# VectorE's weighted sum of three batches back, issued inside the rounds of the decode, and TensorE's side work moved behind unit 5

## What is computed

```python
h = jnp.maximum(_layernorm(x, axis=-1), 0.0)
h = h @ W
e = leaky_relu((h @ a_src)[:, None] + (h @ a_dst)[None, :], 0.2)
attention = softmax(where(adj > 0, e, NEG_INF), axis=1)
x = x + attention @ h
```

## Time and profile before

| | us |
|---|---|
| median of 3 executions | 851.71 (850.29 to 860.48) |
| the profiled execution, its device time | 860.06 |
| span in the profile of it | 858.3 |
| VectorE busy in it | 592.4 |

### The profile page before, as it was taken

The page is one execution under the profiler, slowest core; times in us unless marked ns, Lnnn a source line. Parts: engine busy times, 40 slices in busy tenths (PEclk is TensorE's granted clock), DMA queues, the critical chain, the costliest instruction groups (busy, mean ns, idle before and its releaser), DMA issues.

```text
span 858.3 us, 8941 instructions
## 1 busy us (share of the span) xinstructions
PE 445.4 (52%) x1823; PEld 213.9 (25%) x1855; DVE 592.4 (69%) x3125; ACT 525.0 (61%) x371; POOL 512.0 (60%) x522
## 2 busy tenths in 40 slices
PE   4787555555555546545554545475055567533421
PEld 3652222222222222212122222132022222211221
DVE  7956577777777767566678767767177788755784
ACT  3979777666767667766387777666154877732000
POOL 3745666666656665765655666667636665665571
PEclk9888678677676777766677777777578767765555
DMA  8999999999999999989599999999659799992110
GB/s 339 424 370 419 404 408 408 408 411 407 410 409 409 408 409 405 399 315 393 217 415 411 408 409 408 408 401 409 233 210 394 277 408 409 411 402 92 25 38 11
DMA packets 40903, 299.31 MB, mean 349 GB/s; under 512 B 11052, under 2 KB 14034, under 8 KB 24464
## 3 DMA queue, kind: packets, MB, share of 16 engines
q1 hardware_dynamic: 22976, 276.83, 79.3%
q0 software_dynamic: 15328, 17.58, 6.6%
q10 hardware_dynamic: 2544, 4.33, 1.5%
HBM read 304.31 MB, written 8.65 MB: 365 GB/s over the span
## 4 chain that ended last, share of the span: by engine, by line
DVE 72%; another core or an unknown queue 11%; issue 8%; PE 5%; ACT 2%; DMA 0%; POOLq 0%; DVEq 0%; ACTq 0%
DVE x_all L821 18%; DVE rest L638 5%; DVE words L636 5%; DVE words L640 4%; PE banks L1049 3%; DVE wf L666 2%; DVE top L680 2%; DVE top_bit L662 2%; DVE cand L676 2%; DVE cand L723 1%; DVE one_hot L768 1%; DVE e L785 1%; DVE top_bit L672 1%; DVE top L727 1%
## 5 line engine op out<-in xcount | busy, mean ns | idle before, releaser
L361 POOL DMA_INDIRECT gathered<-table,index x448 | 448.7, 1002 | 295.1 <-DVE index L714 151.4
L467 ACT ACTIVATE mask_buf<-adj_buf,minus_half 128x2048 bf16<-128x2048 int32 x252 | 489.5, 1992 | 141.3 <-issue 56.5
L1049 PE MATMUL banks<-mask_buf,bit_ident 128*128 128x512 bf16 x992 | 316.6, 472 | 37.6 <-issue 24.7
L821 DVE SCALAR_TENSOR_TENSOR x_all<-gathered,weight,x_all 128x128 f32<-128x128 f32 x512 | 157.5, 348 | 16.1 <-DVE x_all L821 7.6
L1049 PEld LDWEIGHTS banks<-mask_buf,bit_ident 128*128 128x128 bf16 x1024 | 113.2, 121 | 203.4 <-issue 137.6
L1061 PE MATMUL banks<-is_wide,before 128*128 128x1 bf16 x64 | 6.9, 176 | 207.9 <-DVE is_wide L751 155.9
L1090 PE MATMUL banks<-x_all,one_hot 128*128 128x128 f32 x128 | 35.4, 368 | 74.1 <-DVE x_all L821 39.0
L481 ACT ACTIVATE prob<-e 128x16 f32<-128x16 f32 x31 | 6.5, 208 | 103.6 <-issue 72.7
L636 DVE MAX8 words<-banks 128x8 f32<-128x512 f32 x64 | 44.3, 693 | 25.4 <-PE banks L1049 18.7
L1061 PEld LDWEIGHTS banks<-is_wide,before 128*128 128x128 bf16 x64 | 4.5, 112 | 227.8 <-DVE is_wide L751 170.8
L640 DVE MAX8 words<-rest 128x8 f32<-128x512 f32 x64 | 44.5, 695 | 2.4 <-DVE rest L638 0.2
(11 more groups left out here) (162 smaller groups left out, 589.4 us busy)
## 6 DMA issues: line engine op xcount, KB each, us to landing
adj_buf<-in_adj SPq DMA_DIRECT2D x128, 2048.0 KB
gathered<-table,index POOLq DMA_INDIRECT x448
table<-gathered ACTq DMA_DIRECT2D x4, 1040.0 KB, 14.0
x_all<-in_x SPq DMA_DIRECT2D x3, 1024.0 KB, 10.8
out<-x_all SPq DMA_DIRECT2D x2, 1280.0 KB
x_all<-in_x SPq DMA_DIRECT2D x2, 512.0 KB, 5.1
out<-x_all SPq DMA_DIRECT2D x1, 1024.0 KB
w_gathered<-table,w_index POOLq DMA_INDIRECT x24
```

The costliest lines, as they stand in the source:

```text
L361: nc.gpsimd.indirect_dma_start(g_cols[buf][:, k, :], None, table, bass.IndirectOffsetOnAxis(index[:, buf, k:k + 1], 0), bounds_check=N, oo ...
L467: nc.scalar.activation(mask_buf[:, u], adj_buf[:, u], ACT.Sign, bias=minus_half[:]).then_inc(mask_ready, 1)
L821: ins = v.scalar_tensor_tensor(at[b], g_view[par][b][:, k, 0:F], weight[:, b, k:k + 1], at[b], ALU.mult, ALU.add)
L1049: ins = mm(bank, bit_ident[:, h * PART_BITS + c], mask_buf[:, u, c * BIT_COLS:(c + 1) * BIT_COLS], start=False, stop=(h == PARTS - 1 and c ...
```

## The change

VectorE: in batches 3 to 29 the exponentials' sum, reciprocal and weights of batch i-3 (`weights`) run between the two `find_words`, each with a step of `logits(i-2)`, under `alone`; the eight pairs (`weighted`) follow `place_wide` as steps beside `decode(i)`. TensorE: records, counts and sums all stand behind unit 5, in that order, ahead of units 6 and 7. ScalarE: `wide_softmax` stands behind unit 7, not 5.

```diff
-                        if u == 5 and i == GROUP_ENDS[g] + 7:
+                        if u == UNITS - 1 and i == GROUP_ENDS[g] + 7:
                             wide_softmax(g)
...
+            def weights(i):
+                two = i % 2
+                dve.wait_ge(exp_ready, i + 1)
+                v.tensor_reduce(max_sum[:, i % BUFS, :, 1], prob[:, two], AX.X, ALU.add)
+                yield
+                v.reciprocal(r4[:], max_sum[:, i % BUFS, :, 1])
+                yield
+                v.tensor_tensor(weight[:], prob[:, two], r4[:].unsqueeze(2).to_broadcast([P, BATCH, SLOTS]), ALU.mult)
+                yield
+
+            def weighted(i):
+                for k in range(SLOTS):
+                    for b in range(BATCH):
+                        row = x_all[:, i * BATCH + b, :]
+                        ins = v.scalar_tensor_tensor(row, g_view[i % BUFS][b][:, k, 0:F], weight[:, b, k:k + 1], row,
+                                                     ALU.mult, ALU.add)
+                    if k == SLOTS - 1:
+                        ins.then_inc(out_ready, 1)
+                    yield
...
+            def both_of(one, other):
+                other = iter(other)
+                for step in one:
+                    next(other, None)
+                    yield
+
+            def one_by_one(one, other):
+                yield from one
+                yield from other
...
                 find_words(i, 0)
                 if i in BY_TILE:
                     decode(i, 0, 1)
-                if i >= SUM_LAG:
                     weighted_sum(i - SUM_LAG, beside=logits(i - LOGITS_LAG))
+                elif i >= SUM_LAG:
+                    alone(both_of(logits(i - LOGITS_LAG), weights(i - SUM_LAG)))
                 elif i >= LOGITS_LAG:
                     alone(logits(i - LOGITS_LAG))
                 find_words(i, 1)
-                decode(i, 1 if i in BY_TILE else 0, BATCH, beside=place_wide(i - COUNT_LAG) if i >= COUNT_LAG else ())
+                if i in BY_TILE:
+                    decode(i, 1, BATCH, beside=place_wide(i - COUNT_LAG))
+                elif i >= SUM_LAG:
+                    decode(i, beside=one_by_one(place_wide(i - COUNT_LAG), weighted(i - SUM_LAG)))
+                elif i >= COUNT_LAG:
+                    decode(i, beside=place_wide(i - COUNT_LAG))
+                else:
+                    decode(i)
...
                 pack(i, 0)
-                if i >= SUMS_LAG:
-                    add_sums(i - SUMS_LAG)
-                for u in (1, 2):
+                for u in range(1, UNITS - 2):
                     pack(i, u)
                 if i >= RECORD_LAG:
                     add_records(i - RECORD_LAG)
-                pack(i, 3)
                 if i >= COUNT_LAG:
                     count_wide(i - COUNT_LAG)
-                for u in range(4, UNITS):
+                if i >= SUMS_LAG:
+                    add_sums(i - SUMS_LAG)
+                for u in range(UNITS - 2, UNITS):
                     pack(i, u)
```

## The result

The changed kernel takes **904.77 us** (median of 4, 904.02 to 908.98), the kernel before beside it 856.10 (median of 4, 850.29 to 866.25): a ratio of **1.060, 95% interval 1.051 to 1.070**, so slower. Ratios compare fast runs alone (here without the one of 866.25, from a slower state), so they differ a little from the quotients of the medians. The forecast was 838 with a range of 818 to 862. The profiled executions are 905.20 and 860.06, with spans of 903.4 and 858.3: 45.1 us to explain.

A forecast was written before the change was run, and what follows sets the result against it. VectorE and the DMA were taken to bound the loop at nearly one pace. Losses falling from 35.2 to 19 us, plus 1 at the start, gave 17 profiled, taken as 13 off 851.7: 838 us, range 818 to 862.

The forecast's parts named there:

- What bounds the kernel: Loop pinned by VectorE and the DMA at nearly one pace, 22.6 us a batch; 35.2 us lost over it.
- Part 1 and 2: Between the two find_words: VectorE's own work takes 4.0 us, TensorE's 5.5, so VectorE waits some 1.5 a batch.
- Part 3: VectorE in decode: pairs cost nothing in held rounds; a batch takes 22.15 us, winning back about 0.45 behind a stall.
- held stretch: Part of VectorE's decode with slow rounds, from about 14 us behind the first gather to 2.1 behind the last.
- held round: VectorE decode round taking far longer than its work; put at 1.70 us without a pair, 1.77 with one.
- Part 4: Batches 13 and 23, behind the wide gathers: GpSimd's pause falls to 0.3 us; 10.5 lost each, bounds 7 and 14.
- the stalls: DMA dips at batches 13 and 23, which took 11.6 and 14.7 us more than 22.6 before the change.
- the sum: Whole kernel: losses of 26 us less 7 won back, 19 against 35.2; with 1 at the start, 17 gained.
- The start: First batches: TensorE reaches units 4 and 5 sooner, a gain of 1 us.
- Part 5: ScalarE's wide_softmax moved behind unit 7: two more masks go first; nothing in the sum, up to 4 us in the range.
- the pairs push the index back: Rival, rounds between L661 and L714: 0.6 us for each pair in a held round, cycle 24.2, 884 us; chance 0.12.
- The lock: Rival: a pair in the held stretch is held to a gather's end, 1.0 us each; cycle 25.6, 930 us; chance 0.03.

The follow-up runs named there:

- e2: Kernel before with only TensorE's and ScalarE's parts of the change, VectorE's order as before; 848.8 us, ratio 1.011 (1.004 to 1.019).
- e4: Kernel before with 24 spare tensor_scalar instructions a batch on VectorE, three in each round of the weighted sum; 914.8 us, one run.
- e5: Kernel before with 24 spare tensor_tensor instructions a batch on VectorE, three in each round of the weighted sum; 925.0 us, one run.
- e9: Whole change with four iotas on GpSimd ahead of its wait for the index, not within the series of gathers; 905.7 us, one run.
- e3: Whole change with nine empty steps between place_wide and the eight pairs, so no pair is issued ahead of the index; 882.7 us, ratio 1.051.
- e1: Changed kernel with TensorE's and ScalarE's loops put back, leaving VectorE's part alone; 996.7 us, ratio 1.191 (1.181 to 1.200).
- e8: Kernel before with 20 spare 128x1 matmuls on TensorE ahead of the counts of wide nodes; 929.2 us, one run.
- e6: Whole change with a GpSimd rest of four iotas between the seventh and eighth gather of each batch; 845.2 us, ratio 0.990 (0.986 to 0.993).
- e12: Whole change without four of the five one-element memsets between the two find_words; 899.8 us, ratio 1.046 (1.043 to 1.049).
- e13: Kernel before with eight spare tensor_tensor instructions a batch on VectorE, one in each round of the weighted sum; 887.8 us, one run.

## Why the prediction was wrong, step by step

- *What bounds the kernel* held as to VectorE. The DMA's 22.6 us a batch was some 0.3 too many (e2); it had been read off batches that VectorE paced.
- *Part 1 and 2* (4.0 and 5.5 us between the two `find_words`) held: 5.62 us, of which 1.89 waiting for TensorE. TensorE's timeline of batch 20 has the terms; counts from 548.89, sums from 549.04, the packs that VectorE waits for from 551.13:

```profile
548.89 0.21 PE L1103 MATMUL banks<-is_wide,before 128*128 128x1 bf16 x2 [13.32 <-issue]
...
549.04 0.77 PE L1132 MATMUL banks<-x_all,one_hot 128*128 128x128 f32 x2
...
551.13 3.19 PE L1091 MATMUL banks<-mask_buf,bit_ident 128*128 128x512 bf16 x7 [0.24 <-issue]
```

- *Part 3 is the step that failed*, in both of its inputs: the place where the held stretch begins and the price of a pair in it. I wrote that four rounds reach 12.9 us and that three to four are then held, at the 1.70 to 1.77 of the earlier trace rows, "a pair costs nothing in a held round". Measured: two rounds fit ahead, since the stretch begins 11.7 to 12.3 us behind the first gather instead of 14.1; held rounds with a pair take 2.83, 2.85 and 2.14 us (559.82, 562.65, 565.50, 567.64), so three are held; four remain, 0.9 each, where I had one or two. (4 - 1.5) x 0.9 = 2.2 us: 22.15 + 2.2 = 24.3, which is the measured batch of 24.26. By an estimate from the same rows each input alone would have lost about one round (4 + 6.0 / 2.61 = 6.3 and 2 + 8.3 / 1.75 = 6.7 done by the end of the stretch, for 7.5); no run parts the two.

  The place of the start was taken as fixed behind the first gather, because it stood there in nearly every batch (the prediction has every one; in a few it began at 14.6 to 17.2 us). In every batch of *one* kernel the same instructions lie ahead of it; that is no evidence that they don't matter.

  The price was misread from rows 6. Their two rounds hold a pair and nothing else, two instructions; the rounds of batch 19 without a pair hold two or three. Neither shows a pair *added* to a round. The trace of before has what was missing (VectorE, batch 19, between the rows):

```profile
505.69 0.19 DVE L665 SCALAR_TENSOR_TENSOR cand<-wi 128x32 f32<-128x32 int32 x1 [1.16 <-DVE top_bit L662]
...
506.41 0.17 DVE L670 TENSOR_SCALAR cand<-cand 128x2 f32<-128x2 f32 x1 [0.42 <-DVE wf L666]
```

  With 504.27 and 508.53 these are held rounds of 1.42, 0.72 and 2.12 us: whole multiples of 0.71. So are the 2.83, 2.85 and 2.14 above and the 1.45 and 1.44 of e4 and e5. Of the 97 spans from one late instruction to the next in the 26 batches of before, 95 lie within 0.05 us of such a multiple, and 63 of 69 after. On average a held round of two instructions takes 1.38 us and one of three 1.88 (before), one of four 2.60 and one of five 3.30 (after). The pair's two instructions thus cost 1.2 to 1.4 us in a held round, where I had nothing and at most 0.6. It is not a price of every instruction: in e4 and e5 rounds of five take 2.0. What sets the 0.71 is open.
- *Part 4*: the stalls cost 35.42 - 22.6 = 12.8 and 34.6 - 22.6 = 12.0 us, inside the bounds of 7 to 14 and above the 10.5 taken. The 37.3 us of batch 23 before had left out the 3.36 us of waiting at its end (40.7 with them), which the sum had among the losses beside it. The index was not ready when GpSimd ended; its pauses there are 5.74 and 4.70 us, where 0.3 was expected (the last two rows; the first two belong to the start, below):

```profile
89.81 0.99 POOL L361 DMA_INDIRECT gathered<-table,index  x1 [0.66 <-issue]
...
121.46 0.99 POOL L361 DMA_INDIRECT gathered<-table,index  x1 [13.73 <-DVE index L714]
...
397.90 0.99 POOL L361 DMA_INDIRECT gathered<-table,index  x1 [5.74 <-DVE index L714]
...
654.14 0.99 POOL L361 DMA_INDIRECT gathered<-table,index  x1 [4.70 <-DVE index L714]
```

- *The start*, "plus 1 in the first batches", had the wrong sign. The first two rows above are batch 1 and 2: TensorE is earlier in batch 1, its index is ready when the gathers of batch 0 end, GpSimd goes on after 0.66 us (3 us before), and the stretch goes on through the second series. VectorE needed 37.8 us for batch 1 instead of 21.5. I had written exactly this mechanism for the stalls and not looked for it at the start. With e9's iotas between the two series it took 20.2 us. How much of the 9.9 us is the change's is open: e4 runs the program of before in its first three batches, and in its execution the pause was 1.1 us and batch 1 took 29.2.
- *Part 5* stands as it was put: nothing in the sum. e2 shows it only together with TensorE's part.
- *The rivals*: "the pairs push the index back" had the right place, and its cycle of 24.2 is what came (chance 0.12). Its 884 lacked the 10 us of the start and counted 10 back in the stalls, which gave 4.8. That its cycle fits is luck: it charged 0.6 us to each pair in a held round, which is half of what the traces show there, and had no earlier start; and e3 shows that taking the pairs away from there does not bring all of the time back. The lock is excluded: the pairs in the rounds take 350 ns each, as before (x432 in 133.3 us).

## What to carry to other kernels

When a wait ends at the same place in every batch, ask what else stands ahead of it in every batch before taking the place as fixed; a rearrangement that makes the start of a batch denser can move it. Where an engine issues a long series of gathers and others stop hearing of finished work, try a pause within the series: here 3 us of rest in each series were worth 60 us to the changed kernel, and together with TensorE's part 1 to 2% over the kernel before. Such a pause is worth what it takes off the engine that sets the pace: look where the held rounds stand afterwards. And an edit with halves on two engines should be costed by halves, since one alone can be far worse (e1) than none.

## What the runs showed of the hardware, and what stays open

- A finished instruction of TensorE reached an idle VectorE 5.8 us late in batch 20 of e3 and 9.5 us late in batch 20 of e8 (10.5 behind the pack's end), while GpSimd issued gathers, and the wait ended between 0.2 us ahead of and 1.4 us behind the last gather's end.
- The stretch comes earlier with more instructions of VectorE, of either kind (e4, e5), or of TensorE (e8). A rest of 3.25 us in the middle of fourteen gathers takes it out of the way of the index and gains 59.5 us, one of 2.0 about half; held rounds remain (e6).
- Within the stretch VectorE's instructions go on at whole multiples of 0.71 us, in the kernels before and after alike (95 of 97 and 63 of 69 spans); a gather starts every 1.30 us there, so it is not the gathers' own beat.
- What fills up, if anything does, is open. So is the law of it: counts of instructions fit the kernels before and after, e4, e5 and e12, and not e13. It was not tried whether fewer gathers, or gathers spaced evenly, do the same as one rest.
- One candidate lies in how the profiler works. The Trainium skill, NOTIFIC — the notification-queue block, section "Overflow: three behaviours, one of which stalls the engine", says that the block which writes the engines' records holds its producers back when it fills up inside. No run here shows that; every execution in this document has a span and a clock of its own, so none tells what the kernel does unrecorded.
